# Splitting the closing LayerNorm of the expert blocks over two rounds, and moving the scaling of tokens and the key gate into the projection

## What is computed

```python
x = x + _layernorm(attn(_layernorm(x), Wq, Wk, Wv, gq, gk, Wo, bo, ln_w, ln_b))
x = x + _layernorm(ffn(_layernorm(x), gamma, beta, router_w, gate_up_w, down_w, shared...))
# attn(x): 16 heads of 8
x_norm = (x - mu) / sqrt(var + eps) * ln_w + ln_b
q, k = l2norm(heads(x_norm @ Wq)), l2norm(heads(x_norm @ Wk));  v = heads(x @ Wv)
resonance = sigmoid((q k^T - 0.29514) * 15)
modulation = resonance * (q . gq)[:, None] * (k . gk)[None, :]
return (modulation @ v) @ Wo + bo
# ffn: top 2 of 8 experts (128 -> 512 -> 128, SwiGLU), plus one shared expert of width 128
```

## Time and profile before

| | |
|---|---|
| median of three runs | 756.92 us (754.97 to 757.45) |
| the profiled execution, its own time | 754.22 us |
| its span, first to last instruction | 752.4 us |
| mean granted TensorE clock | 0.937 |
| PE busy | 628.7 us (84%) |
| ACT busy | 569.3 us (76%) |
| DVE busy | 431.5 us (57%) |
| POOL busy | 161.8 us (22%) |

### The profile page before, as it was taken

The page is one execution under the profiler, slowest core; times in us unless marked ns, Lnnn a source line. Parts: engine busy times, 40 slices in busy tenths (PEclk is TensorE's granted clock), DMA queues, the critical chain, the costliest instruction groups (busy, mean ns, idle before and its releaser), DMA issues.

```text
span 752.4 us, 15215 instructions
## 1 busy us (share of the span) xinstructions
PE 628.7 (84%) x5866; PEld 252.6 (34%) x5866; DVE 431.5 (57%) x1126; ACT 569.3 (76%) x661; POOL 161.8 (22%) x149
## 2 busy tenths in 40 slices
PE   3477999999889999998889999989899999317840
PEld 2232211113214444442134444421344444106740
DVE  6997176811734555527655455376455553686963
ACT  2579899998998888879988888899788888004520
POOL 1123000000042122140412222404121123142442
PEclk9679999999999999999999999999999999657995
DMA  9500002600045445120444442103544431038931
GB/s 329 206 29 30 33 4 82 271 22 8 1 149 171 124 142 147 48 61 1 150 162 123 140 147 72 50 12 122 157 144 120 132 95 41 16 112 274 291 106 38
DMA packets 47640, 82.02 MB, mean 109 GB/s; under 512 B 5457, under 2 KB 25169, under 8 KB 47569
## 3 DMA queue, kind: packets, MB, share of 16 engines
q1 hardware_dynamic: 45088, 76.31, 31.4%
q0 software_dynamic: 2048, 4.20, 1.9%
q10 hardware_dynamic: 432, 0.54, 0.3%
HBM read 64.58 MB, written 16.45 MB: 108 GB/s over the span
## 4 chain that ended last, share of the span: by engine, by line
PE 29%; DVE 8%; ACT 5%; issue 4%; DMA 2%; POOL 2%; SPq 0%; POOLq 0%; DVEq 0%
PE AV L783 11%; PE UO L857 6%; PE S L769 6%; ACT res L658 4%; PE GB L857 3%; DVE work L1253 2%; DVE work L1260 1%; PE UO L806 1%; DMA gu_ring<-gu_dram 1%; POOL y_tok L564 1%; POOL xs_dram L551 1%; DVE work L1386 1%; DMA xs_dram<-xrow,slot 1%; PE UO L852 1%; DVE work L1291 0%
## 5 line engine op out<-in xcount | busy, mean ns | idle before, releaser
L658 ACT ACTIVATE res<-S 128x1024 f32<-128x1024 f32 x478 | 464.2, 1046 | 56.9 <-PE S L769 55.0
L783 PE MATMUL AV<-res,vg 128*8 128x512 f32 x2048 | 294.2, 599 | 0.9 <-DVE coll L1139 0.9
L769 PE MATMUL S<-qT,kT 32*128 32x512 f16 x956 | 140.6, 388 | 19.0 <-ACT res L658 14.9
L579 POOL TENSOR_TENSOR work<-work 128x512 f32<-128x512 f32 x64 | 82.0, 1282 | 274.5 <-DVE work L1260 274.4
L769 PEld LDWEIGHTS S<-qT,kT 32*128 32x128 f16 x956 | 37.2, 91 | 245.8 <-ACT res L658 197.6
L632 ACT ACTIVATE work<-work,scl 128x512 f32<-128x512 f32 x64 | 46.2, 722 | 44.9 <-DVE work L1253 44.8
L551 POOL DMA_INDIRECT xs_dram<-xrow,slot x32 | 31.6, 987 | 216.6 <-issue 216.6
L1253 DVE TENSOR_SCALAR work<-GB,scl 128x512 f32<-128x512 f32 x56 | 45.3, 809 | 52.0 <-PE GB L857 52.0
L1260 DVE SCALAR_TENSOR_TENSOR work<-work,scl,UO 128x512 f32<-128x512 f32 x56 | 41.7, 745 | 44.1 <-PE UO L857 43.7
L1404 DVE TENSOR_SCALAR gate_q<-GB 128x512 f32<-128x512 f32 x16 | 11.1, 692 | 88.4 <-PE GB L794 88.4
L1272 DVE TENSOR_TENSOR hid_lo<-work,hid_hi 128x512 f16<-128x512 f32 x64 | 53.8, 841 | 3.2 <-ACT hid_hi L648 1.6
(11 more groups left out here) (210 smaller groups left out, 611.9 us busy)
## 6 DMA issues: line engine op xcount, KB each, us to landing
gu_ring<-gu_dram SPq DMA_DIRECT2D x60, 512.0 KB, 3.6
dn_ring<-dn_dram SPq DMA_DIRECT2D x60, 256.0 KB, 3.3
work<-in_gu SPq DMA_DIRECT2D x8, 512.0 KB, 10.4
gu_dram<-gu_ring SPq DMA_DIRECT2D x8, 512.0 KB, 2.7
ys_dram<-work SPq DMA_DIRECT2D x60, 64.0 KB, 2.6
work<-in_down SPq DMA_DIRECT2D x8, 256.0 KB, 10.9
dn_dram<-dn_ring SPq DMA_DIRECT2D x8, 256.0 KB, 2.9
work<-xs_dram SPq DMA_DIRECT2D x4, 448.0 KB, 5.0
```

The lines of the kernel that those rows point to most:

```text
L579: nc.gpsimd.tensor_tensor(hid[u % 2], prod[u % 2], sg[u % 2], ALU.mult).then_inc(hid_ready, 1)
L658: nc.scalar.activation(res[:, k % 2, 2 * half:2 * half + 2, :].rearrange("p h t -> p (h t)"), score_banks(i, k, half).rearrange("p h t -> ...
L769: mm = nc.tensor.matmul(banks[:, j % 2, :], kT[r, g, s * P:(s + 1) * P], qT[r, g, :], start=True, stop=True)
L783: mm = nc.tensor.matmul(AV[32 * j:32 * j + HD, :], vg[:, s, G * g + j, :], res[:, k % 2, j, :], start=s == 0, stop=s == ST - 1)
```

## The change

In the prologue, `tokens` now applies the factor of the second normalisation at once. The layer norm's weight is multiplied into a copy of Wq and Wk (`w_scaled`), and the bias part is added in PSUM by a matmul of its own, before the scaled one. The key gate becomes 16 further columns of the projection, filled on the device by `set_up`; v is projected by a third matmul, and its missing factor goes into the small tile gk_s. DVE's scaling pass and its two gate passes over the block go away, and q and k are normalised in place in the copied rows (`heads`). ACT takes the squares straight from its own copies, and `square(0)` comes ahead of `tokens(1)` in the list.

In the expert blocks, `finish` is split: `sum_up` (the weighted sums and their statistics) runs in round 14, ahead of the up part of unit 0, and the rest stays in round 17. After the rounds both parts follow each other as before.

```diff
+NQKV = 3 * D + H
-OUT_ROUND, ..., SHARED_ROUND, FINISH_ROUND = 1, 7, 8, 10, 13, 17
+OUT_ROUND, ..., SHARED_ROUND = 1, 7, 8, 10, 13
+SUM_ROUND, FINISH_ROUND = 14, 17
-PROLOGUE = [("tokens", 0), ("project", 0), ("tokens", 1), ("square", 0), ("project", 1), ("high", 0),
+PROLOGUE = [("tokens", 0), ("project", 0), ("square", 0), ("tokens", 1), ("project", 1), ("high", 0),
...
             def project(b):
-                    act.wait_ge(vg_ready, b - 1)
+                    act.wait_ge(lo_ready, 2 * b - 2)
...
             def square(b):
-                act.wait_ge(qk_ready, b * SUB + SUB)
+                act.wait_ge(raw_ready, b * SUB + SUB)
...
-            nc.tensor.matmul(GB[:, 0:2 * D], lnb_all[:], w_qkv[:, 0:2 * D], start=True, stop=True).then_inc(bias_mm, 1)
...
             def project_qkv(b, turned):
-                    nc.tensor.matmul((GB, OB)[j % 2][:, 0:3 * D], hT[:, j * P:(j + 1) * P], w_qkv[:],
-                                     start=True, stop=True).then_inc(qkv_mm, 1)
+                    bank, h, n = (GB, OB)[j % 2], hT[:, j * P:(j + 1) * P], 2 * D + H
+                    nc.tensor.matmul(bank[:, 0:n], lnb_all[:], w_qkv[:, 0:n], start=True, stop=False)
+                    nc.tensor.matmul(bank[:, 0:n], h, w_scaled[:], start=False, stop=True)
+                    nc.tensor.matmul(bank[:, n:NQKV], h, w_qkv[:, n:NQKV], start=True, stop=True).then_inc(qkv_mm, 1)
...
             def set_up():
-                dve.wait_ge(bias_mm, 1)
-                v.tensor_copy(b_qk[:], GB[:, 0:2 * D]).then_inc(setup, 1)
-                v.tensor_scalar(w_qkv[:, 0:2 * D], w_qkv[:, 0:2 * D], col(V_LNW), None, ALU.mult).then_inc(setup, 1)
+                dve.wait_ge(in_qkv, 16)
+                link(v.tensor_tensor(gk_prod[:], w_qkv[:, D:2 * D]..., gk, ALU.mult))
+                link(v.tensor_reduce(w_qkv[:, 2 * D:2 * D + H], gk_prod[:], AX_X, ALU.add))
+                v.tensor_scalar(w_scaled[:], w_qkv[:, 0:2 * D + H], col(V_LNW), None, ALU.mult).then_inc(setup, 1)
...
             def unit(b):
-                wait(dve, hi_ready, b * 2)
-                wait(dve, lo_ready, b * 2)
-                for j in range(SUB):
-                    dve.wait_ge(raw_ready, b * SUB + j + 1)
-                    v.scalar_tensor_tensor(...)            # raw * fac2 + b_qk
-                dve.wait_ge(qk_ready, b * SUB + SUB)
-                link(v.tensor_tensor(gk_prod[:], unit_k, gk, ALU.mult))
-                link(v.tensor_reduce(gk_s[:], gk_prod[:], AX_X, ALU.add))
...
-                link.count(v.tensor_tensor(gk_s[:], gk_s[:], rn[:, NQK // 2:NQK], ALU.mult))
-                v.tensor_tensor(both, both, rn_t[:]..., ALU.mult).then_inc(unit_ready, 1)
+                v.tensor_tensor(heads[b % 2], heads[b % 2], rn_t[:]..., ALU.mult).then_inc(unit_ready, 1)
+                link(v.tensor_tensor(gk_heads, raw[b % 2][:, :, 2 * D:2 * D + H], rn_heads[:, :, H:2 * H], ALU.mult))
+                link(v.tensor_tensor(gk_heads, gk_heads, fac2[...]..., ALU.mult))
...
-            def finish(i, link):
+            def sum_up(i, link):
                 dve.wait_ge(y_gathered, i * 2 * SUB * 16)
...
                 stats(link, lambda j: acc[:, j, :])
+
+            def finish(i, link):
                 variance(link, s_var, 0, SUB, False)
...
+                        if k == SUM_ROUND and i > 1:
+                            sum_up(i - 1, link)
                         if k == FINISH_ROUND and i > 1:
                             finish(i - 1, link)
```

More of the change, by code:

```diff
@@ L206, in build @@
             x_sb = scratch("x_sb", [P, ST, D])
-            w_qkv = scratch("w_qkv", [P, 3 * D])
+            w_qkv = scratch("w_qkv", [P, NQKV])
+            w_scaled = scratch("w_scaled", [P, 2 * D + H])
             lnb_all = scratch("lnb_all", [P, P])
-            b_qk = scratch("b_qk", [P, 2 * D])
             ssq = scratch("ssq", [P, NQK])
@@ L218, in build @@
         raw = [m.rearrange("p (s n) -> p s n", s=SUB)
-               for m in (pwork[:, TB:4 * TB], coll[:, 0:3, :].rearrange("p g t -> p (g t)"))]
+               for m in (pwork[:, TB:TB + SUB * NQKV], coll[:].rearrange("p g t -> p (g t)")[:, 0:SUB * NQKV])]
+        heads = [m[:, :, 0:2 * D].rearrange("p s (n d) -> p s n d", d=HD) for m in raw]
         q_out = y_tok[:].rearrange("p n s d -> p (n s d)").bitcast(F16).rearrange("p (g t) -> p g t", g=NG)
-        qk = pwork[:, 4 * TB:6 * TB].rearrange("p (w n) -> p w n", w=2)
         sq = pwork[:, 6 * TB:8 * TB].rearrange("p (n d) -> p n d", d=HD)
@@ L599, in project @@
                 if b >= 2:
-                    act.wait_ge(vg_ready, b - 1)
+                    act.wait_ge(lo_ready, 2 * b - 2)
                 for j in range(SUB):
                     act.wait_ge(qkv_mm, b * SUB + j + 1)
-                    nc.scalar.activation(raw[b % 2][:, j, :], (GB, OB)[j % 2][:, 0:3 * D], ACT.Copy).then_inc(raw_ready, 1)
+                    nc.scalar.activation(raw[b % 2][:, j, :], (GB, OB)[j % 2][:, 0:NQKV], ACT.Copy).then_inc(raw_ready, 1)
             def square(b):
-                act.wait_ge(qk_ready, b * SUB + SUB)
-                nc.scalar.activation(sq, qk.rearrange("p w n -> p (w n)").rearrange("p (n d) -> p n d", d=HD),
-                                     ACT.Square).then_inc(sq_ready, 1)
+                act.wait_ge(raw_ready, b * SUB + SUB)
+                nc.scalar.activation(sq.rearrange("p (s n) d -> p s n d", s=SUB), heads[b % 2], ACT.Square).then_inc(sq_ready, 1)
             def high_parts(b):
@@ L613, in high_parts @@
                 for w in (0, 1):
-                    nc.scalar.activation(split[:, w, :, 0, :], qk[:, w, :].rearrange("p (n d) -> p n d", d=HD),
-                                         ACT.Copy).then_inc(hi_ready, 1)
+                    nc.scalar.activation(split[:, w, :, 0, :].rearrange("p (s h) d -> p s h d", s=SUB),
+                                         heads[b % 2][:, :, w * H:(w + 1) * H, :], ACT.Copy).then_inc(hi_ready, 1)
             def turn(b):
@@ L722, in project_qkv @@
                 if b == 0:
-                    pe.wait_ge(setup, 5)
+                    pe.wait_ge(setup, 4)
                 wait(pe, qk_copied, 4 * turned)
@@ L1109, in low_parts @@
             def low_parts(b):
-                for w, of in ((0, unit_q), (1, unit_k)):
+                for w in (0, 1):
                     dve.wait_ge(hi_ready, b * 2 + w + 1)
-                    v.tensor_tensor(split[:, w, :, LOW_SLOT[w], :], of, split[:, w, :, 0, :], ALU.subtract).then_inc(lo_ready, 1)
+                    hi, lo = (split[:, w, :, n, :].rearrange("p (s h) d -> p s h d", s=SUB) for n in (0, LOW_SLOT[w]))
+                    v.tensor_tensor(lo, heads[b % 2][:, :, w * H:(w + 1) * H, :], hi, ALU.subtract).then_inc(lo_ready, 1)
             dve.wait_ge(in_x, 16)
@@ L1454, in _ @@
             shared_in(NB)
+            sum_up(NB - 1, link)
             finish(NB - 1, link)
@@ L1460, in _ @@
                 drain(NB, n)
+            sum_up(NB, link)
             finish(NB, link)
```

37 lines of the change are left out of this document (16 added, 21 removed).

## The result

The changed kernel takes 748.01 us (median of four runs, 747.79 to 748.68), the kernel before 756.07 in the runs beside it (four, 754.97 to 757.45). The ratio is 0.9894, interval 0.9874 to 0.9913: between 6.6 and 9.5 us less. The forecast was 3.5 less, and 748.5 the low end of its range. The direction was right, the size was not.

The account below looks back on a forecast made before the run. The prediction took DVE to bound the prologue and stall PE in round 20 of blocks 2 and 3. The finish's 5.5 less the prologue's 2.0 gave 3.5 us off 756.92: 753.4 us, range 748.5 to 758.5.

Parts of the forecast that it names:

- the prologue's sum: All prologue terms together: between +0.2 and +4.5 us, taken as +2.0, about as long as before.
- Blocks 0 and 1: Prologue: the longer PE projection makes the high parts of block 0 start 0.5 to 2.2 us later.
- The earlier bank copies: Prologue: ACT's bank copies of block 0 no longer stand behind a square waiting for DVE, giving back 1.4 us.
- Block 2: Prologue: one to two projection subtiles show, 0.6 us at full clock or 2.0 at half.
- Block 3: Prologue: two to four subtiles cost 1.3 to 2.5 us, less 0.8 for the square: +0.5 to +1.7.
- PE takes DVE's place as the bound: Prologue: PE and ACT bound it where DVE did; DVE's 4.03 us a block become idle time.
- The finish: Rounds of blocks 2 and 3: splitting finish gives back 3.9 to 7.0 us, taken as 5.5.
- The first part at nothing: Round 14: the moved sums fit DVE's idle time and cost nothing, with 1.4 us a block as the other bound.
- eat the gain: Rival: half clock in blocks 1 and 2 makes the prologue +4.5, net -1 to +0.6, about 756.5 us; chance 0.20.
- every projection ran at half clock: Rival, slower: a block's projection takes 9.4 us, the prologue is 7.8 us longer, 764 us in all; chance 0.10.
- Late tiles in place of the copy: Rival: late DMA in blocks 2 and 3 leaves 1.6 us of the split's gain, no change, 757.3 us; chance 0.08.
- DVE stays what matters: Rival: PE's columns hide in its holes, blocks 1 to 3 of the prologue gain 10.5 us, 741 us; chance 0.07.

Follow-up runs that it names:

- e2: The changed kernel with both parts of finish in round 17, so the prologue's change alone: 757.08 us, the kernel before 756.46.
- e11: The changed kernel unaltered, a second profiled execution: 747.25 us.
- e7: The changed kernel with the second part of finish in round 23 instead of 17: 759.90 us, the kernel before 756.62.
- e8: The changed kernel with both parts of finish in round 14: 754.56 us, the kernel before 756.62.
- e3: The changed kernel with the projection's bias matmul issued twice in each subtile: 756.86 us, the kernel before 756.46.
- e5: The changed kernel without the projection's bias matmul, so the bias of q and k is left out: 743.23 us, the kernel before 756.62.
- e12: The kernel before unaltered, a second profiled execution: 757.1 us.
- e4: The changed kernel with DVE's sum of squares done twice in each block: 750.02 us, the kernel before 756.46.
- e10: The changed kernel with square(0) put back behind tokens(1): 748.39 us, the kernel before 755.41.
- e1: The kernel before with the split finish alone: 749.38 us, the kernel before 756.46.
- e6: The kernel before with the arithmetic of finish left out of the rounds, one addition in its place: 749.17 us, the kernel before 756.62.
- e9: The changed kernel with the norm's weight and bias applied by ACT in a second token copy, no bias matmul: 746.00 us, the kernel before 755.41.

## Why the prediction was wrong, step by step

**The step that failed is the prologue's sum**, in two of its terms: the price of a subtile in the blocks 0 and 1, and the cost of block 2. The sum was put at +2.0, with +0.2 as its low end; the marks give -1.4. That is 3.4 of the 4.6 us between the forecast and the median difference (8.1 - 3.5). By its own terms, on the high parts of the two first executions:

- *Blocks 0 and 1*, +0.5 to +2.2: measured 26.84 - 27.55 = -0.7. A subtile was priced at 1.38 us at full clock (0.56, 0.56 and 0.27) and took 1.14 (0.46, 0.46 and 0.22, from start to start). The price came from the 0.75 for 384 columns and the 0.27 for 128. The 0.75 starts at the first matmul of a run (54.38, right behind value matmuls). In after the first matmul of a run goes on after 0.56, be it behind a wait (21.51 to 22.07) or behind value matmuls (51.07 to 51.63), and the same 272 columns after 0.46 within the run. So 0.10 of the 0.75 is paid once for a run, and I had spread it over all columns: 384 of them at the pace of 1.14 for 672 would take 0.65, by estimate. With the dearer 128 columns that makes 4 x 0.24 = 1 us for four subtiles. And block 1 ran at full clock all through, which the forecast had as the better of two cases. The window row of the changed kernel over it (columns as in the earlier trace rows):

```profile
21.50:26.20 4.70, 4.69 (x24) 4.01 (x24) 4.29 (x13) 1.51 (x3) 0.00 (x0) 1.00 1.07 377
```

- *The earlier bank copies*, -1.4: from the high parts to the first bank copy it was 33.55 - 27.55 = 6.0 before and is 31.63 - 26.84 = 4.8 now, -1.2. Right.
- *Block 2*, +0.6 to +2.0: from the high parts of block 1 to those of block 2, 13.5 before and 12.8 now, -0.7. The first subtile ran at half clock (37.65 to 40.05) and the second mostly at full (40.05 to 41.39), between the two cases, but the raw copies ended at 44.37 and the square followed at once, where it had waited for the scaling until 46.28. That square stands between the two marks, so its 0.8, which the prediction took off in block 3, was won here. And the next turn and values ran at full clock, where before they had half. One stretch of before and then the same work in after:

```profile
51.00:53.00 2.00, 1.88 (x12) 0.95 (x16) 1.80 (x7) 0.78 (x3) 0.00 (x0) 0.50 0.19 72
```

```profile
49.00:51.00 2.00, 1.79 (x16) 0.64 (x16) 1.86 (x5) 1.24 (x3) 0.00 (x0) 1.00 0.20 78
```

  That the denser projection ahead of it is enough to keep the clock up doesn't hold: in e2, with the same prologue, this work has 0.50 (49.10 to 51.10), and in e11 too (48.90 to 50.90).
- *Block 3*, +0.5 to +1.7: 13.6 before, 15.0 now, +1.4. Within the range, though without the 0.8 of the square the forecast would have been +1.3 to +2.5.

The two first executions flatter the first term. Over the nine executions with one prologue or the other (four and five, as above) the means of the same four terms are -0.2, -1.4, -0.6 and +1.4, with small rests of -0.2 and -0.3 between and behind them: -1.4 in all. The first term varies with the moment at which block 0's projection gets the full clock: its last subtile starts at 17.76 in e7 and at 19.23 in e8, and the high parts of block 0 start at 26.57 and 28.04.

That PE takes DVE's place as the bound was right, as e3 and e5 show, and so is the wait of DVE for ACT.

**The finish**, 5.5 out of 3.9 to 7.0: the three blocks together gave 6.1. The parts differ from those I named. Block 3 gave 4.5 (23.8 to 19.3), as "nearly certain". Block 2 gave 3.8 (23.2 to 19.4), more than its upper bound of 2.79: the late load that I had left standing there is gone from block 2, and the excess of the second execution of before was 4.75. Against that block 1 lost 2.1 (19.4 to 21.5) to a late load that no step of mine has. "The excess is 2.79 and 4.23, together 7.0, and that is all that the split can give back" was read from one execution; e12 has 4.75 and 4.54. The second part, 3.75 in the prediction, took 5.48 (521.19 to 526.67), since POOL's product now meets it (last section). So DVE was done after the transposes at 525.64 and not before them; it cost nothing, since value and score matmuls fill PE up to the gate matmuls.

**The first part at nothing** was right: gate_q and the collapse still wait for PE. The part is also shorter at its new place, 514.53 to 518.18, 3.65 instead of 5.25. The bound of 1.4 a block did not come.

**The late tile** explains why e2 shows no gain: its prologue is 0.1 better than the mean of before, and block 1 loses 2.5 (it has no late tile in block 2, but both stalls of the finish). What makes the load late isn't settled. It stood in block 1 in the seven executions with the changed projection as it is (after, e2, e4, e7, e8, e10, e11), in block 2 in the four with the old prologue (before, e1, e6, e12) and in e9, in block 3 in e3, and nowhere in e5. Two kinds are seen. In block 1 of after SP issues the load only 2.96 us after POOL's last scatter (219.36 to 222.32), against 1.29 in its block 2 (372.38 to 373.67). In block 2 of before the load is issued in time, but its three issues take 2.17 instead of 1.48:

```profile
371.72 2.17 SPq L468 DMA_DIRECT2D work<-xs_dram  x3
```

So it goes with the program and not with chance alone; the cause stays open, no run here tells apart by which timing.

**The rivals.** None came. The prologue did not eat the gain, and not every projection ran at half clock: block 1 had 1.00. Late tiles in place of the copy was half true: they stand in one block of most executions. "DVE stays what matters" promised 741 and the prologue that ends 2 us earlier; e5 reaches 743 only without the bias matmul. Of the signs of being right, the gate matmuls of unit 1 (527.38, right behind the scores) and the marks of the blocks 2 and 3 (13.99 and 13.82 from the gate of round 15) came; the 1.3 to 1.5 us a subtile and the later prologue did not.

## What to carry to other kernels

Price a run of matmuls by the distance from start to start of rows that follow each other without a wait, at the granted clock of that place; the first row of a run carries a cost that is paid once (0.10 us here), and a price that spreads it over all columns was 1 us too high for a block of four subtiles. Work that stands in one piece on an engine's list can be hidden by cutting it to fit two holes, and e6 shows how to learn what the hiding can give at most: leave the work out. When a stall is removed, look for the second wait that stood under it, and read its size from more than one execution.

## What the runs showed of the hardware

**Some DVE instructions are held up while POOL multiplies.** Before, one of the eight multiply-adds in `finish` took 1.9 us, beside POOL's product of 1.28 us; the eight took 3.89, and in round 14, away from that product, they take 2.33. In the changed kernel the product meets a multiply of 4 elements in each partition instead (L372, 1.82 us, and 0.16 for the same form at L373). In e2, with the sums back in round 17, the eight take 3.88 again:

```profile
525.58 3.88 DVE L1373 SCALAR_TENSOR_TENSOR work<-y_tok,twt,work 128x128 f32<-128x128 f32 x8
...
526.58 1.28 POOL L579 TENSOR_TENSOR work<-work 128x512 f32<-128x512 f32 x1
```

So some 1.6 us are lost in each of these meetings, to a long instruction as to a short one. Not every instruction is held: in the trace of before the clip of one input (L1253) takes 0.80 to 0.81 us whether it meets POOL's product or not, and the subtraction of hid_lo with two inputs (L1272) takes 0.69 alone and 0.68 to 1.64 when it meets it. The Trainium skill, GPSIMD Engine Reference, 1. Specifications, says that GpSimd shares its SBUF interfaces with VectorE and contends with DVE instructions in a 2-port perf mode or with two SBUF inputs; the trace agrees, the multiply-add, L372 and the subtraction have two inputs, and adds the size. A cast of one input (L1270) is held too, 0.42 alone and up to 0.99; whether it runs in such a mode, the trace does not show.

**Transposes and the clock.** In the prediction a rule stood beside the stretch of the earlier trace rows: the Trainium skill, TensorE: Matmul & The Clock Gate, Part 4: PE-mode transpose, has transposes not counted as busy. After PE had idled 4.25 us, the same 32 transposes ended differently. In after the clock stays at the lower level of 1.2 GHz over them and the turn of the next tokens behind them takes 1.08 us. In e2 it is at that level from 32.10 to 35.30, over the transposes, and at 2.4 GHz from 35.50, before PE did anything else, and the same turn takes 0.63. The stretch in after:

```profile
30.50:35.80 5.30, 3.79 (x32) 3.17 (x32) 4.95 (x15) 3.88 (x4) 0.52 (x1) 0.50 0.24 99
```

And in e2:

```profile
31.52 1.45 PE L747 MATMUL UO<-id,pwork 128*128 128x128 f16 x16 [4.25 <-POOL pwork L538]
33.34 1.92 PE L747 MATMUL UO<-id,pwork 128*128 128x128 f16 x16 [0.36 <-ACT qT L623]
36.42 0.63 PE L712 MATMUL UO<-const_sb,tok 128*128 128x128 f32 x4 [1.16 <-issue]
```

```profile
32.10:35.30 3.20, 2.80 (x25) 2.15 (x22) 2.99 (x9) 2.85 (x3) 0.00 (x0) 0.50 0.11 44
35.50:36.40 0.90, 0.00 (x0) 0.01 (x1) 0.83 (x3) 0.82 (x1) 0.00 (x0) 1.00 0.82 332
```

There the rule doesn't hold: PE ran nothing but these transposes from 31.52 to 36.42, and the clock rose. e11 does the same. When the clock rises and falls in the prologue differs between executions of one code, and the prologue's end with it: by 2.6 us over the five (76.40 to 78.99). Of that, 1.4 us lie behind the last high parts: from there to the prologue's end e2 takes 11.03 us, with a clock of 0.50 from 73.10 to 76.20, and the other four take 9.65 to 9.69.
